# Spiking attention block with a mixture of experts: the first layer norm's scaling by two ScalarE instructions ahead of W2's result, in place of two on VectorE

## What is computed

```python
def lif_step(v, x_t):
    v = v + (x_t - v) * TAU_INV
    s = spike(v - V_TH)
    v = v * (1.0 - s)
    return (v, s)
...
    # srwkv_forward: R, K, V = x @ Wr.T, x @ Wk.T, x @ Wv.T; per time step
    h = h * DECAY + k * v
    y = r * h
...
    attn_out = jnp.einsum('tbd,ed->bte', yT, Wo)
    x1 = layernorm(residual + attn_out, ln1_g, ln1_b)
    h1 = jnp.einsum('btd,fd->btf', x1, W1) + b1
    s1 = lif_scan(h1)
    h2 = jnp.einsum('btf,df->btd', s1, W2) + b2
    ffn_out = lif_scan(h2)
    return layernorm(x1 + ffn_out, ln2_g, ln2_b)
```

## Time and profile before

| | |
|---|---|
| median of 3 runs | 1044.15 us (1040.43 to 1044.51) |
| the profiled execution | 1044.85 us, of which its instructions span 1043.0 us |
| mean granted PE clock | 0.961 |
| PE / PEld busy | 93% / 90% |
| DVE busy | 93% |
| ACT busy | 52% |
| POOL busy | 56% |

### The profile page before, as it was taken

One profiled execution on the slowest core, in us unless ns is written; L12 is line 12 of the kernel. 1 busy time (PEld: TensorE's weight loads), 2 busy tenths in 40 slices (PEclk: granted clock), 3 DMA queues, 4 the chain that ended last, 5 costly groups with the idle time before them and its releaser, 6 DMA issues.

```text
span 1043.0 us, 22651 instructions
## 1 busy us (share of the span) xinstructions
PE 965.0 (93%) x7552; PEld 935.1 (90%) x7552; DVE 965.0 (93%) x3860; ACT 540.0 (52%) x1256; POOL 580.4 (56%) x720
## 2 busy tenths in 40 slices
PE   5567788999999999999999999999999999899884
PEld 5567777999999999999999999999999999899884
DVE  5888897999999999999999999999999999998765
ACT  4333323456655555555665555555566555455351
POOL 1000122666666676776666666677666666665451
PEclk8878878999999999999999999999999999999998
DMA  4310111344555444544455545454445554446662
GB/s 158 99 52 31 31 41 41 70 91 87 110 102 112 102 104 97 105 101 91 88 108 102 112 102 107 98 102 102 90 87 108 102 112 92 98 95 115 132 126 65
DMA packets 53109, 98.30 MB, mean 94 GB/s; under 512 B 5888, under 2 KB 5888, under 8 KB 52992
## 3 DMA queue, kind: packets, MB, share of 16 engines
q0 software_dynamic: 31392, 57.16, 32.3%
q1 hardware_dynamic: 16992, 31.30, 9.3%
q10 hardware_dynamic: 4608, 8.39, 2.1%
HBM read 31.29 MB, written 8.39 MB: 38 GB/s over the span
## 4 chain that ended last, share of the span: by engine, by line
PE 79%; DVE 14%; ACT 3%; issue 2%; POOL 1%; DMA 0%; POOLq 0%; DVEq 0%; ACTq 0%
PE ps_e L349 30%; PE ps_proj L349 12%; PE ps_proj L404 11%; PE ps_proj L419 9%; PE ps_attn L385 6%; PE ps_proj L425 5%; DVE U L723 3%; DVE V L730 3%; PE ps_zx L393 2%; DVE h L774 1%; PE ps_attn L393 1%; DVE stats L804 1%; POOL s L1161 1%; DVE x_lo L852 1%; ACT x L577 1%
## 5 line engine op out<-in xcount | busy, mean ns | idle before, releaser
L349 PE MATMUL ps_e<-we_hi,x_hi 128*128 128x256 f32 (+1 forms) x1024 | 296.3, 289 | 5.1 <-ACT odd_sum L596 3.2
L349 PE MATMUL ps_e<-we_lo,x_hi 128*128 128x256 f32 (+1 forms) x1024 | 287.6, 281 | 0.0
L349 PE MATMUL ps_e<-we_hi,x_lo 128*128 128x256 f32 (+1 forms) x1024 | 287.5, 281 | 0.0
L730 DVE SCALAR_TENSOR_TENSOR V<-U 128x256 f32<-128x256 f32 (+5 forms) x656 | 249.2, 390 | 0.7
L723 DVE SCALAR_TENSOR_TENSOR U<-V,U 128x256 f32<-128x256 f32 (+5 forms) x656 | 238.0, 373 | 0.9
L559 ACT ACTIVATE U<-ps_proj,cst 128x256 f32<-128x256 f32 x320 | 135.5, 480 | 175.9 <-PE ps_proj L404 98.2
L1147 POOL TENSOR_SCALAR veps<-mv 128x2 f32<-128x2 f32 x128 | 53.9, 421 | 284.1 <-DVE mv L810 284.1
L349 PEld LDWEIGHTS ps_e<-we_hi,x_hi 128*128 128x128 f32 x1024 | 193.5, 189 | 10.6 <-ACT odd_sum L596 8.4
L1161 POOL TENSOR_SCALAR s<-U 128x256 fp32r<-128x256 f32 x208 | 192.5, 951 | 7.7 <-DVE V L730 7.7
L349 PEld LDWEIGHTS ps_e<-we_hi,x_lo 128*128 128x128 f32 x1024 | 193.9, 189 | 0.1
L349 PEld LDWEIGHTS ps_e<-we_lo,x_hi 128*128 128x128 f32 x1024 | 193.1, 189 | 0.0
(11 more groups left out here) (87 smaller groups left out, 2187.7 us busy)
## 6 DMA issues: line engine op xcount, KB each, us to landing
acc<-term POOLq DMA_DIRECT2D x93, 256.0 KB, 3.7
odd_sum<-term POOLq DMA_DIRECT2D x93, 256.0 KB, 3.4
xt<-x_T SPq DMA_DIRECT2D x33, 256.0 KB, 3.0
xa<-x_tok SPq DMA_DIRECT2D x32, 256.0 KB, 3.8
xb<-cst SPq DMA_DIRECT2D x32, 256.0 KB, 2.3
xb<-x_tok POOLq DMA_DIRECT2D x32, 256.0 KB, 6.0
out<-res ACTq DMA_DIRECT2D x32, 256.0 KB, 2.1
term<-w SPq DMA_DIRECT2D x8, 256.0 KB, 5.2
```

The costliest lines, as they stand in the source:

```text
L349: mm = pe.matmul(dst, lhs, rhs, start=(i == 0), stop=(i == n - 1))
L730: v.scalar_tensor_tensor(out=V[:, c0:c1], in0=u, scalar=THRESHOLD, in1=u, op0=ALU.is_lt, op1=ALU.mult).then_inc(done, 1)
```

## The change

The two DVE instructions of the scaling go. In their place DVE makes `shift` with one small instruction (`mean_shift`), in full beats one slot earlier (slot 12 for 13; in FILL the slot stays 9), and ACT scales x1n in place with two instructions, placed after gexp and ahead of W2's result in its stream. LN1_STEPS falls from 7 to 6, and a new semaphore x1n_ready tells PE that x1n may be transposed.

```diff
-              ln1_sum=8, ln1_stats=(9, 9), ln1_aggr=10, ln1_norm=13, x1_low=19,
+              ln1_sum=8, ln1_stats=(9, 9), ln1_aggr=10, ln1_norm=12, x1_low=19,
...
-        Y_STEPS, LN1_STEPS, LN2_STEPS, LN3_STEPS, GATE_STEPS, FIN_STEPS = 2, 7, 8, 5, 15, 7
+        Y_STEPS, LN1_STEPS, LN2_STEPS, LN3_STEPS, GATE_STEPS, FIN_STEPS = 2, 6, 8, 5, 15, 7
...
-                    pe.wait_ge(ln1_steps, b.value(LN1_STEPS, LAG_Y, LN1_STEPS))
+                    pe.wait_ge(x1n_ready, b.value(1, LAG_Y, 1))
                     transpose4(ps_attn, lambda k, j: x1n[:, j, k * P:(k + 1) * P], x1T_done)
...
+            def norm_x1(b):
+                act.wait_ge(ln1_steps, b.value(LN1_STEPS, LAG_Y, LN1_STEPS))
+                normalised(0, x1n, x1n).then_inc(x1n_ready, 1)
+
...
                     nc.scalar.activation(gexp[:], gdiff[:], ACT.Exp).then_inc(gexp_ready, 1)
+                if b.has(LAG_Y):
+                    norm_x1(b)
                 if b.has(LAG_S):
...
-            def normalise(b, ln, dst, src, steps, lag):
-
-                dve.wait_ge(rstd_ready[ln], b.value(2, lag, 2))
-                for j in range(TILES):
-                    v.tensor_scalar(dst[:, j, :], src[:, j, :], mv[ln][:, j, 0:1], rstd[ln][:, j:j + 1],
-                                    ALU.subtract, ALU.mult).then_inc(steps, 1)
...
                     if slot == at["ln1_norm"]:
-                        normalise(b, 0, x1n, x1n, ln1_steps, LAG_Y)
+                        mean_shift(b, 0, ln1_steps, LAG_Y)
```

More of the change, by code:

```diff
@@ L257, in build @@
         y_steps, attn_done, ln1_steps = sem("y_steps"), sem("attn_done"), sem("ln1_steps")
-        x1T_done, x1_ready = sem("x1T_done"), sem("x1_ready")
+        x1n_ready, x1T_done, x1_ready = sem("x1n_ready"), sem("x1T_done"), sem("x1_ready")
         x1_hi_ready, x1_lo_ready = sem("x1_hi_ready"), sem("x1_lo_ready")
```

## The result

The median of the changed kernel is 1037.49 us (14 executions, 1034.04 to 1041.20), that of the kernel before in the same comparison 1041.88 us (14 executions, 1040.43 to 1044.51). The ratio is 0.9951 with an interval of [0.9938, 0.9965]. 2.3 us of that lie in the base: the forecast started from the 1044.15 us of three runs, and the kernel before has a median of 1041.88 here. Both belong to the result: the change gains somewhere between nothing and some 0.5%, and much of what follows is about why.

A forecast was written before the change was run, and what follows sets the result against it. Full beats were taken as bound by the chain PE, ACT, DVE x_lo, PE, not DVE alone. Terms 0 (full beats) + 1.27 + 0.80 (beats 1, 2) - 0.54 (beat 31) = +1.5 on 1044.15 gave 1045.6 us, range 1041 to 1050.

The forecast's parts named there:

- one more Wo product: Filling beats: one Wo product, or equal matmuls, changes clock level, widening the range by 2.06 us either way.
- +2.07: Beats 1 and 2: ACT's norm queues behind the rkv reads, costing 2.07 us together, bounds 0 and 2.6.
- The saving turns into a wait of about 0.5 us in each of the 24 full beats: Full beats: DVE's saved work becomes waiting for ACT's x; 13 us of work saved, 0 us on the path.
- The first rival: Full beats: DVE sets the pace, so each gains 0.55 us; 1035 to 1038 us, chance 0.08.
- the second: Full beats: ACT's slower pair lies on PE's path, costing 0.6 us a beat; 1060 us, chance 0.07.
- Beats 3 to 6 on the norm's own account: Filling beats 3 to 6: x1n stays early for PE's transpose, 0.59 us early in tightest beat 5; cost 0.
- Beat 31: Beat 31: DVE is last at x1_low and keeps its saving, a gain of 0.54 us, bounds 0 and 0.65.
- +1.27 and +0.80: Beat 1: PE's transpose 1.27 us later, all on the path; beat 2: x_lo's end 0.80 us later.
- at about 40.56: Beat 1: ACT begins the norm at 40.56 us behind the third rkv read, and ends it 1.12 us later.
- No DMA and nothing on SP or POOL moves: Full beats: other engines keep their times, with POOL's rstd asked for at the same moment; no size given.
- The fourth rival: Beats 1 or 2: the clock falls because PE idles 1.3 us longer, costing 2 to 4 us; 1048 to 1050, chance 0.12.
- My own last line: Filling beats: a total change of more than 4 us would prove the prediction wrong and would be the clock.

The follow-up runs named there:

- the first comparison: Changed kernel against the kernel before, 14 executions each: medians 1037.49 and 1041.88 us, ratio 0.9951 [0.9938, 0.9965].
- e3: Kernel before plus extra matmuls at the head of PE's beats (60 in beat 1, 30 in beats 2 to 6): 1037.03 us, ratio 0.9954.
- e4: Changed kernel plus extra matmuls at the head of PE's beats (60 in beat 1, 30 in beats 2 to 6): 1033.26 us, ratio 0.9919.
- after: First profile of the changed kernel, against the profile of the kernel before: profiled execution 1037.87 us, instructions spanning 1036.0 us for 1043.0.
- e10: Kernel before with the change in beats 3 to 32 only, beats 1 and 2 scaling on DVE: 1041.10 us, ratio 0.9984.
- f5: Kernel before, unchanged, profiled one more time: single time 1042.57 us.
- e2: Kernel before with the change in beats 7 to 32 only, filling beats as before: 1040.51 us, ratio 0.9993.
- f3: Kernel before, unchanged, profiled one more time: single time 1041.03 us.
- the second comparison: Same changed kernel run again against the kernel before: medians 1037.62 and 1040.95 us, ratio 0.9993 [0.9973, 1.0013].
- e1: Kernel before with the change in the six filling beats only, beats 7 to 32 scaling on DVE: 1042.92 us, ratio 0.9997.
- e8: Repeat of the kernel before with the change in beats 1 to 6 only: 1038.91 us, ratio 0.9995.
- f1: Kernel before, norm on DVE, with PE waiting in beats 1 and 2 for two unused ACT instructions before x1n's transpose: 1039.06 us, ratio 0.9971.
- f2: Changed kernel plus 10 extra matmuls ahead of x1n's transpose in beats 1 and 2: 1040.78 us, ratio 0.9984.
- e6: Kernel before plus extra matmuls at beat heads (beats 1 to 6), ahead of x1n's transpose (1, 2) and W1's waits (1 to 5): 1035.10 us, ratio 0.9945.
- e9: Kernel before with POOL's x_lo instruction moved behind the next beat's y in beats 1 to 5: 1038.10 us, ratio 0.9955.

## Why the prediction was wrong, step by step

**The steps that failed.** The forecast was +1.5 us, and the first comparison has -4.4. A term of the range and one of the sum failed. The clock was allowed "one more Wo product", 2.06 us either way; between the two profiles it moved beats 3 to 6 by 5.1 us, and the same program by 4 to 5. And beats 1 and 2 were put at +2.07; between the two profiles they are 1.6 us shorter, and the clock's fall and a GpSimd instruction had moved there together with the norm. A third part, 2.3 us, is the base of three runs, which the larger sample did not confirm.

**Full beats: right.** "The saving turns into a wait of about 0.5 us in each of the 24 full beats": it did, 16.8 us of waits for 2.9 in 23 beats, or 0.60 more a beat. Beats 7 to 30 take 693.2 to 694.6 us in all 20 profiles, and old and new form stand at both ends of that. PE's wait at the low half is 0.20 us a beat for 0.21. ACT's pair took 1.09 us for the 1.12 assumed, and the margin of 1.1 us stood. The first rival, that DVE sets the pace, fell; so did the second, that ACT's slower pair does. The rule of the Trainium skill by which the first was argued ("Perfetto Trace Analysis", Identifying the Most-Contended Engine) named DVE by its occupancy, and here the trace does not bear it out: 13.2 us less of DVE in 660 us shortened nothing, since the chain there lies on PE.

**Beats 3 to 6 on the norm's own account: right**, no wait for x1n appeared there.

**Beat 31: right.** Forecast -0.54; measured 27.48 to 26.91, -0.57, and 26.90 to 26.92 in every profile with the new form against 27.33 to 27.60 with the old.

**Beats 1 and 2: the term was mis-sized.** Forecast +1.27 and +0.80, measured in e3 and e4 up to the end of x_lo +0.97 and +0.08. In after itself PE starts the transpose of beat 1 9.73 us after Wo's product starts (41.12 - 31.39), for 8.68 before: +1.05. The steps that were off are ACT's start "at about 40.56", 8.77 us after Wo's start where 8.59 was measured (39.98 - 31.39), and the pair, 1.08 us for 1.12. For beat 2 I had only the timeline with Wo's product at the half level. With the product at the full level the norm is not queued behind the reads but waits for shift, and the 0.5 us by which DVE is later than x cover it; after even takes 0.25 us less than e10 there, which has the norm on DVE and the same level (11.82 for 12.07).

**Two effects behind it were missing.** The prediction followed ACT's lateness to DVE's x_lo and stopped. "No DMA and nothing on SP or POOL moves" was written of full beats. In beat 1 it does not hold: where W1 falls to half, ACT's x_hi of the tokens comes later, POOL's x_lo goes off DVE's updates of h, and the way from x_lo to the next Wo falls from 9.82 to 8.70 us. It is W1's fall that goes with this and not the norm: e10 and f5, with the norm on DVE and W1's fall, have 8.79, and before, e2 and f3, without the fall, 9.81 to 9.82. And Wo's product in beat 2 runs at the full level, 1.8 us shorter. In the table, beats 1 and 2 take a mean of 45.5 us with the norm on ACT (6 profiles, 44.7 to 46.3) and 46.1 with it on DVE (5 profiles, 44.3 to 47.4): -0.6 where I had +2.07. The difference lies within the scatter of single profiles and mixes two things. Among the profiles with W1's fall alone, the norm on ACT has 45.5 and on DVE 44.6 (e10 and f5): +0.9, the sign of the forecast. The three on DVE without the fall have 47.0. So by these few profiles the norm costs time there, and the fall, which all profiles with the norm on ACT have, gives back more.

**The clock: the mechanism was seen and its size missed.** The fourth rival had the clock fall because PE idles longer in beats 1 and 2, and priced it as a loss of 2 to 4 us. It does fall, in W1 of beat 1, and the profiles with that fall have the shorter beats 1 and 2 (44.6 for 47.0 us with the norm on DVE): a gain and not a loss. The range took "one more Wo product" of 2.06 us either way. What it should have taken is the second fall in W1 of beats 3 to 5, 4 to 5 us, which the profile of before has and other profiles of the same kernel have not. My own last line, that a change of over 4 us in the filling beats "would be the clock", is what happened.

**The sum after the fact.** From the means of the table, beats 1 and 2 give -0.6, with the scatter just said, and beat 31 -0.6, -1.2 us or -0.1%, which fits the second comparison (-0.07%, to -0.27%) and not the first (-0.49%, at least -0.35%).

**What stays open.** Whether the change makes the good pattern in beats 3 to 5 more frequent: one of four profiles of the changed kernel has it, and one of three of the kernel before, which says nothing. The single executions speak for it (18 of 26 under 1038 us, for 6 of 43 of the kernel before in the same two comparisons), e1 and e8 with the same filling beats less so, and f1, where added idle time gave 0.3%, has an interval that ends at 0.9991. The later comparisons each ran on another chip, and for the first the chip is not recorded; the chip is a rival for what differs between the first and the second, and it was not tested. That W1's fall in beat 1 is caused by the longer idle time is supported by 8 of 8 against 2 of 6 profiles; f2, which should have taken it away, halved it. The mean gain of the change is therefore bracketed by the two comparisons and not settled.

## What to carry to other kernels

Moving work off the engine with the highest busy share gains only in beats where that engine is the last at the point where it meets the others; of the 32 beats with this norm that was shown for beat 31, and in the full beats 13 us of saved work became 13 us of waiting. Where PE idles for some microseconds in every beat, one profile shows one of several clock patterns: take more than one profile of the kernel before, and put the difference between them into the range. Such idle time is itself something to fill, and an instruction on GpSimd can be moved to where VectorE waits: both together with the change from beat 3 on gave 1.0% (1030.75 us, [0.9854, 0.9945]). Each of the two by itself gave 0.5% (e6 and e9), so that figure needs no share of the change.

## What the runs showed of the hardware

The same program gave profiles of 1036.0 and 1041.2 us span, by where the granted clock of TensorE was at its half level in the filling beats (0.87 and 0.84 in the mean). 210 extra matmuls in six beats, into a bank that nobody reads then, made the kernel 0.46% faster [0.9930, 0.9977]. In its profile Wo's products behind them ran at the full level, 2.4 GHz (1.9 to 2.0 us for 3.8), and PE was busier and ended sooner (138.44 us busy in 155.31, for 134.08 in 167.26). And with 1.3 us of added idle time ahead of the transpose in each of beats 1 and 2, a kernel came out 0.3% faster, [0.9951, 0.9991]; its profile shows W1 later, Wo's product of beat 2 at the full level and the GpSimd instruction out of VectorE's way; that these are the cause is argued from one profile.

Four small updates on VectorE (128x32, two SBUF inputs) took 1.91 us for 0.87 while a GpSimd instruction of 1.27 us ran beside them. Moving that one instruction gave 0.45% [0.9928, 0.9981].
